# Block attention scores in 64x64 tiles, sums in three groups, later sums in the order, and norm scaling on GpSimd

## The reference

```
x = layernorm(x + blocksparse_attention(x))      # 16 heads of 8, blocks of 64 tokens
hn = layernorm(x)*g + b ; q,k,v = hn@wq+bq, ...   # 16 heads of 8, full 1024x1024 scores
x1 = x + attention(q,k,v)@wo + bo
hn2 = layernorm(x1)*g + b ; idx = argmax(hn2@gate_w + gate_b)
x = layernorm(x + x1 + expert[idx](hn2))
```

## Time and profile before

| | |
|---|---|
| median of 3 runs | 940.32 us (936.14 to 944.61) |
| profiled execution | 937.35 us, its span 935.6 us |
| busy share of the span | PE 81%, DVE 60%, ACT 47%, POOL 22% |
| mean granted PE clock | 0.788 |
| chain that ended last | PE 65%, DVE 18%, issue 5%, POOL 4%, ACT 4%, DMA 3% |

### The profile page before, as it was taken

One profiled execution on the slowest core, in us unless ns is written; L12 is line 12 of the kernel. 1 busy time (PEld: TensorE's weight loads), 2 busy tenths in 40 slices (PEclk: granted clock), 3 DMA queues, 4 the chain that ended last, 5 costly groups with the idle time before them and its releaser, 6 DMA issues.

```text
span 935.6 us, 17249 instructions
## 1 busy us (share of the span) xinstructions
PE 762.3 (81%) x6594; PEld 343.4 (37%) x6594; DVE 565.6 (60%) x941; ACT 443.0 (47%) x826; POOL 203.7 (22%) x460
## 2 busy tenths in 40 slices
PE   4299999999999999977789999987999987305950
PEld 2135655556555565531122212131212122205950
DVE  3253344334554344579987899979789941623745
ACT  2024233333334334327767787866777886002621
POOL 5213420000223342011213410002100000063650
PEclk9557676658657776569989999999999999556985
DMA  4411111212111111111101111110111124013103
GB/s 120 67 18 19 19 19 19 26 19 30 19 19 19 19 19 19 19 15 18 17 10 17 18 22 22 26 14 11 16 18 20 18 78 126 0 40 87 34 32 90
DMA packets 28699, 28.88 MB, mean 31 GB/s; under 512 B 4592, under 2 KB 23824, under 8 KB 28624
## 3 DMA queue, kind: packets, MB, share of 16 engines
q1 hardware_dynamic: 27216, 24.96, 15.4%
q0 software_dynamic: 1408, 2.89, 0.9%
HBM read 9.35 MB, written 5.53 MB: 16 GB/s over the span
## 4 chain that ended last, share of the span: by engine, by line
PE 65%; DVE 18%; issue 5%; POOL 4%; ACT 4%; DMA 3%; SPq 1%; POOLq 0%; ACTq 0%; DVEq 0%
PE PO L1101 23%; PE RB L1138 22%; PE EX L1146 11%; DVE NM L874 11%; ACT PR L732 3%; PE EX L1058 2%; POOL sorted_rows L661 2%; PE RB L1190 1%; PE RB L1115 1%; POOL results L681 1%; PE EX L1197 1%; DVE ST L823 1%; DMA QKT<-QS 1%; PE RB L1089 1%; DVE X L843 1%
## 5 line engine op out<-in xcount | busy, mean ns | idle before, releaser
L874 DVE TENSOR_REDUCE NM<-RB 128x1 f32<-128x1024 f32 (+2 forms) x416 | 433.2, 1067 | 239.7 <-PE RB L1138 229.7
L732 ACT ACTIVATE PR<-EX 128x512 f32<-128x512 f32 (+1 forms) x736 | 383.1, 586 | 300.2 <-PE EX L1146 299.0
L1138 PE MATMUL RB<-QKT 48*128 48x512 bf16 (+4 forms) x1248 | 313.2, 339 | 55.8 <-DVE NM L874 35.5
L1146 PE MATMUL EX<-QKT 51*128 51x512 bf16 (+2 forms) x1536 | 305.6, 309 | 10.3 <-ACT PR L732 6.9
L1101 PE MATMUL PO<-PR,VB 128*32 128x512 f32 (+3 forms) x3072 | 253.1, 440 | 0.1
L1138 PEld LDWEIGHTS RB<-QKT 48*128 48x128 bf16 (+1 forms) x1248 | 94.0, 103 | 286.1 <-DVE NM L874 142.9
L1146 PEld LDWEIGHTS EX<-QKT 51*128 51x128 bf16 (+1 forms) x1536 | 99.4, 111 | 114.7 <-ACT PR L732 69.5
L1101 PEld LDWEIGHTS PO<-PR,VB 128*32 128x32 f32 x3072 | 94.6, 128 | 51.0 <-issue 35.8
L637 POOL COPY VB<-VST 128x128 f32<-128x128 f32 (+1 forms) x64 | 18.7, 292 | 340.4 <-PE PO L1101 327.7
L647 POOL CAST MS<-NM 128x16 bf16<-128x16 f32 x32 | 6.3, 198 | 169.3 <-DVE NM L874 142.0
L755 ACT COPY QS<-QS 128x1156 f32 x12 | 13.8, 1155 | 57.8 <-DVEq L965 43.1
(11 more groups left out here) (158 smaller groups left out, 510.7 us busy)
## 6 DMA issues: line engine op xcount, KB each, us to landing
QKT<-QS SPq DMA_DIRECT2D x64, 192.0 KB
QS<-in_L_ffn_w_dram SPq DMA_DIRECT2D x1, 2048.0 KB, 9.3
QS<-in_L_ffn_w_dram SPq DMA_DIRECT2D x4, 512.0 KB, 9.5
sorted_rows<-PR SPq DMA_DIRECT2D x3, 516.0 KB, 10.1
QKT<-sorted_rows SPq DMA_DIRECT2D x3, 516.0 KB, 5.6
QKT<-MT SPq DMA_DIRECT2D x64, 6.0 KB
CTX<-results SPq DMA_DIRECT2D x2, 512.0 KB, 5.1
X<-_attn_hidden_states_dram SPq DMA_DIRECT2D x2, 384.0 KB, 4.1
```

Of the source, the lines that this page charges most:

```text
L732: nc.scalar.activation(PR[:, at % RING, h, 0:n], bank(key)[:, 0:n], ACT.Exp).then_inc(s_aread, 1)
L874: nc.vector.tensor_reduce(NM[v % 2][:, h, tiles[0]:tiles[-1] + 1], ps, AX_X, ALU.max, negate=True).then_inc(s_dread, 1)
L1138: ins = pe.matmul(spread(ps[r0:r1, c:c + of[1] * of[3]], of), columns(v, h, 0, ROWS6, (l0, 1, 0, ln)), columns(v, h, 1, ROWS6, of), start= ...
L1146: ins = pe.matmul(spread(ps[r0:r1, c:c + of[1] * of[3]], of), columns(xv, xh, 1, ROWS9, (l0, 1, 0, ln)), columns(xv, xh, 0, ROWS9, of), st ...
```

## The change

- Block layer: each MAX matmul of 128 queries becomes two of 64 queries (array columns 0 to 63, and 64 to 127), and the 64-wide window pieces are joined with their neighbours where the columns of `QKT` allow it. Each EXP matmul that was 128 wide becomes two of 64. All score matmuls of that layer are 64x64.
- Block layer: the last three of five groups of sums become one, behind the last EXP step.
- Both layers: `ready` is one beat later. In the full layer the sums so stand between the two beats of a pair.
- SCALE goes from DVE to POOL for the five passes inside the attention layers (40 instructions); DVE keeps the last one.
- A wait of EXP for a free slot of `PR` now names the last group that reads it.

```diff
--- before.py
+++ after.py
@@ -1,4 +1,6 @@
 from contextlib import ExitStack
+
+from itertools import zip_longest
 
 import numpy as np
 
@@ -85,16 +87,29 @@
 
     L = Layer()
     t7 = (TT - 1) * P
-    L.max_acts = [dict(tiles=(0,), n=1024, mms=[(ALL, k * 512, (0, P), (k * 512, 1, 0, 512)) for k in range(2)])]
+
+    def window(j, off, col):
+
+        blk, rows = 2 * j + off // BLK, UPP if off else LOW
+        query, c = (j * P + off, BLK), block_col(blk)
+        if j == TT - 1:
+            near = [(P, (block_col(13), 1, 0, P) if off == 0 else (block_col(2), 2, block_col(1) - block_col(2), BLK))]
+        elif block_col(blk - 1) == c - BLK:
+            near = [(P, (c - BLK, 1, 0, 3 * BLK))]
+        else:
+            near = [(P, (block_col(blk - 1), 1, 0, BLK)), (P + BLK, (c, 1, 0, 2 * BLK))]
+        return [(rows, col, query, (0, 1, 0, P))] + [(rows, col + c0, query, of) for c0, of in near]
+
+    def turns(f):
+
+        return [m for pair in zip_longest(f(0), f(BLK)) for m in pair if m]
+
+    L.max_acts = [dict(tiles=(0,), n=1024, mms=[(LOW if off == 0 else UPP, k * 512, (off, BLK), (k * 512, 1, 0, 512))
+                                                for k in range(2) for off in (0, BLK)])]
     for j in range(1, TT - 1, 2):
-        L.max_acts.append(dict(tiles=(j, j + 1), n=320, mms=[m for i in (0, 1) for m in [
-            (ALL, 512 * i, ((j + i) * P, P), (0, 2, (j + i) * P, P)),
-            (LOW, 512 * i + 2 * P, ((j + i) * P, BLK), (block_col(2 * (j + i) - 1), 1, 0, BLK)),
-            (UPP, 512 * i + 2 * P, ((j + i) * P + BLK, BLK), (block_col(2 * (j + i) + 2), 1, 0, BLK))]]))
-    L.max_acts.append(dict(tiles=(TT - 1,), n=256, mms=[
-        (ALL, 0, (t7, P), (0, 1, 0, P)),
-        (LOW, P, (t7, BLK), (block_col(13), 1, 0, P)),
-        (UPP, P, (t7 + BLK, BLK), (block_col(2), 2, block_col(1) - block_col(2), BLK))]))
+        L.max_acts.append(dict(tiles=(j, j + 1), n=320, mms=[m for i in (0, 1) for m in turns(
+            lambda off: window(j + i, off, 512 * i))]))
+    L.max_acts.append(dict(tiles=(TT - 1,), n=256, mms=turns(lambda off: window(TT - 1, off, 0))))
 
     def single(j, col):
 
@@ -121,6 +136,9 @@
                 [m for j in range(1, 5) for m in single(j, 2 * P + (j - 1) * BLK)])
     ends = dict(n=P, mms=[m for j in (5, 6) for m in single(j, (j - 5) * BLK)])
     L.exp_steps = [first[0], odd, first[1], even, own, rest, ends]
+    for st in L.exp_steps:
+        st["mms"] = [half for rows, c, (l0, ln), of in st["mms"] for half in
+                     ([(LOW, c, (l0, BLK), of), (UPP, c, (l0 + BLK, BLK), of)] if rows == ALL else [(rows, c, (l0, ln), of)])]
     L.exp_acts = [(0, 1), (2, 3), (4, 5), (6,)]
 
     def both(f):
@@ -135,12 +153,12 @@
                                          (h, 0, 2, (2 * P, P), "full", 6, 0), (h, 1, 3, (448, BLK), "low", t1, 448),
                                          (h, 0, 2, (3 * P, P), "full", 7, 0), (h, 1, 3, (448, BLK), "upp", TT - 1, 448),
                                          (h, 0, 3, (0, 384), "full", 0, P)])),
-        dict(last=4, mms=both(lambda h: [(h, j % 2, 4, ((j - 1) * P, P), "full", j, j // 2 * P) for j in range(1, 5)])),
-        dict(last=5, mms=both(lambda h: [(h, j % 2, 5, ((j - 5) * P, P), "full", j, j // 2 * P) for j in (5, 6)] +
-                              [x for a, b_ in ((1, 2), (3, 4))
-                               for pair in zip(single_v(h, 5, a, 2 * P + (a - 1) * BLK),
-                                               single_v(h, 5, b_, 2 * P + (b_ - 1) * BLK)) for x in pair])),
-        dict(last=6, mms=both(lambda h: [x for pair in zip(single_v(h, 6, 5, 0), single_v(h, 6, 6, BLK)) for x in pair]))]
+        dict(last=6, mms=both(lambda h: [(h, j % 2, 4, ((j - 1) * P, P), "full", j, j // 2 * P) for j in range(1, 5)]) +
+             both(lambda h: [(h, j % 2, 5, ((j - 5) * P, P), "full", j, j // 2 * P) for j in (5, 6)] +
+                  [x for a, b_ in ((1, 2), (3, 4))
+                   for pair in zip(single_v(h, 5, a, 2 * P + (a - 1) * BLK),
+                                   single_v(h, 5, b_, 2 * P + (b_ - 1) * BLK)) for x in pair]) +
+             both(lambda h: [x for pair in zip(single_v(h, 6, 5, 0), single_v(h, 6, 6, BLK)) for x in pair]))]
     L.kinds = ["full", "low", "upp"]
     return L
 
@@ -214,7 +232,7 @@
                 acts.append((beats[i], 4, "EXP", li, u, (j, h)))
                 i += 1
             for e in steps:
-                ready[e] = beats[i + 1] + 0.4
+                ready[e] = beats[i + 2] + 0.4
         acts += [(ready[gr["last"]], 5, "AV", li, u, g) for g, gr in enumerate(L.av_groups)]
         exp_end.append(ready[L.av_groups[-1]["last"]] + 0.2)
         if u % 2:
@@ -415,7 +433,7 @@
 
         def av_group_of(li, e):
 
-            return [i for i, gr in enumerate(LAYERS[li].av_groups) if gr["last"] >= e][0]
+            return max(i for i, gr in enumerate(LAYERS[li].av_groups) if any(m[2] == e for m in gr["mms"]))
 
         def piece(li, b, k):
 
@@ -614,6 +632,12 @@
                     n = 2 * u + k if li == 1 else 4 + u
                     pool.wait_ge(s_var, n + 1)
                     root_steps(pool, nc.gpsimd, s_newton, 4 * ROOT_STEPS * n, VE[:, 0:TT], RD[:, 0:TT], SD[:, 0:TT])
+                if kind == "SCALE" and (li, u) != (2, 1):
+                    src, dst = ((X, X1[:]), (X1, X[:]))[k[0]] if li == 1 else (X, HN2[:, :, 0:HS])
+                    for t in (2 * k[1], 2 * k[1] + 1):
+                        g = u * TT + t
+                        nc.gpsimd.tensor_scalar(dst[:, g, :], src[:, g, :], MV[:, t, 0:1], RD[:, t:t + 1],
+                                                ALU.subtract, ALU.mult).then_inc(s_norm, 1)
                 if kind == "AFFINE" and (li, u) != (2, 1):
                     n, row = (2 * u + 1, 0) if li == 1 else (4 + u, 2)
                     if li == 1 and u == 0:
@@ -828,19 +852,15 @@
                         dve.wait_ge(s_dve, chain[0])
                         link(nc.vector.tensor_scalar(VE[:, 0:TT], MV[:, 0:TT, 1], EPS, None, ALU.add))
                         root_guess(VE[:, 0:TT], RD[:, 0:TT], SD[:, 0:TT]).then_inc(s_var, 1)
-                if kind == "SCALE":
-                    n, src, dst = 2 * u + k[0], (X, X1)[k[0]], (X1, X)[k[0]]
-                    if li == 2:
-                        n, dst = 4 + u, HN2[:, :, 0:HS]
-                    if (li, u) != (2, 1):
-                        dve.wait_ge(s_newton, 4 * ROOT_STEPS * (n + 1))
-                    elif k[1] == 0:
+                if kind == "SCALE" and (li, u) == (2, 1):
+                    n = 4 + u
+                    if k[1] == 0:
                         dve.wait_ge(s_var, n + 1)
                         root_steps(dve, nc.vector, s_dve, chain[0], VE[:, 0:TT], RD[:, 0:TT], SD[:, 0:TT])
                         chain[0] += 4 * ROOT_STEPS
                     for t in (2 * k[1], 2 * k[1] + 1):
                         g = u * TT + t
-                        nc.vector.tensor_scalar(dst[:, g, :], src[:, g, :], MV[:, t, 0:1], RD[:, t:t + 1],
+                        nc.vector.tensor_scalar(HN2[:, g, 0:HS], X[:, g, :], MV[:, t, 0:1], RD[:, t:t + 1],
                                                 ALU.subtract, ALU.mult).then_inc(s_norm, 1)
                 if kind == "AFFINE" and (li, u) == (2, 1):
                     dve.wait_ge(s_norm, TT * (4 + u) + 4 * k + 4)
```

## The result

| | before | after |
|---|---|---|
| median, same chip | 938.39 us (4 runs) | 866.64 us (860.91 to 871.08, 4 runs) |
| ratio | | 0.9222, 95% interval 0.915 to 0.9295 |
| profiled execution, its span | 937.35, 935.6 us | 871.08, 869.3 us |

What follows compares the result with a forecast made beforehand. PE's list was taken to bound the block layer, and PE, DVE and ACT together the full layer. Terms -72 - 2 + 3 - 3 - 6 = -80 us against 937.35 gave 857, forecast 860 us; range 836 to 900.

Steps and rivals of the forecast that it cites:

- PE's list sets the block layer: Block layer before the change: 53 shape changes at 0.12 us plus 19,200 columns give 17.4 of a unit's 18.83 us.
- its 11.6: Block layer rival: PE alone sets the unit at 11.6 us, 72 us less, 788; chance 1%.
- The load takes over as the bound at 10.9 us from MT to MAX: Block layer, first stretch of a unit: loads issued behind the MT copies keep it at 10.9 us or more.
- The size of it: Block layer: 15 units of 16.4 us plus 6 us for four heavy units, 252 instead of 324, minus 72 us.
- The second stretch near the low clock: Block unit from MAX to the next MT: 5.0 us, near the low level since PE has just idled; 6.85 before.
- The low clock stays (rival, 881): Block layer rival: PE idles for the load, clock stays low, 17.8 us a unit, 21 us more; chance 14%.
- Between the layers: +3 forecast: Between the layers: MAX 64x128 alternating with EXP 64x64 adds 6,300 columns and loses 15 shape changes, plus 3 us.
- Sums in the full layer: -3 forecast: Full layer: later sums save a little under 0.3 us a unit at MT, nothing in the loop; minus 3 us.
- Norms: -6 forecast: Full layer: scalings leave DVE, 4.9 us in twelve beats plus 1.1; 0.36 us each on POOL; minus 6 us.
- Matmul issue as the bound (rival, 902): Block layer rival: at 0.066 us an instruction a unit takes 19.2 us, 42 us more; chance 3%.
- Sums starving DVE in the full layer (rival, 980): Full layer rival: sums between the beats make each pair wait 1.0 us, 120 us more; chance 4%.
- Before the first MT: -2 forecast: Before the block layer: 13 MAX steps lose 31 shape changes (3.7 us), of which DVE allows 2; minus 2 us.

Runs made afterwards that it cites:

- E1: Kernel before, with only the block layer's MAX and EXP matmuls made 64x64 as in the change: 879.22 us.
- E3: Changed kernel with the loads planned 9.5 instead of 6.0 ahead, so on SP they stand before the MT copies: 828.50 us.
- E10: Changed kernel with early loads, halved MAX matmuls in the first full unit and the block layer's sums in five groups: 793.2 us.
- E7: Kernel before, with the loads planned 9.5 instead of 6.0 ahead: 940.84 us, ratio 1.001 to 1.009.
- E6: Changed kernel with the block layer's sums in five groups again: 863.13 us.
- E5: Changed kernel with the MAX matmuls of the full layer's first unit also cut into 64-wide halves: 849.98 us.
- E2: Changed kernel with all norm scalings back on DVE: 870.88 us.
- E4: Changed kernel with the sums at their old beat in both layers: 878.10 us.
- E8: Changed kernel with early loads, halved MAX matmuls in the first full unit and the first norm's scalings on DVE: 814.58 us.
- E9: Changed kernel with early loads and halved MAX matmuls in the first full unit, scalings as in the change: 819.62 us.

## Why the prediction was right, point by point

- **PE's list sets the block layer, and array shapes are its cost.** Shown in the main: E1 changes nothing but the tiles and gains 57.8 of the layer's 59.6 us. How much of it is shape changes, how much columns and how much the clock (0.66 before, 0.72 in E1) is not taken apart. The count of columns and shapes holds to 1.1 us of PE's busy time in the unit of the earlier trace rows, but falls 2.2 us short at full clock (E3, E10), so that E3's 11.38 us meets its 11.6 by luck.
- **The load takes over as the bound at 10.9 us from MT to MAX.** Shown by the unit above (10.89) and by E3 and E7 together: the same edit takes 38 us from the change and none from the kernel before. Six of the fourteen first stretches came in at 10.8 to 10.9.
- **The size of it.** -72 was forecast, -59.6 came, and the failing term is the pair of stretches: 10.9 and 5.5 us were taken, 11.56 and 5.98 were measured as means over 14 units. That is 1.1 us a unit, 17 in all, of which the separate term for heavy units (6) covered a part. A cost that the forecast did not have is PE waiting for DVE (17.9 us over the layer, 3.5 before). I had let DVE bound only the second stretch, and had not asked what the merged sums do to it. E6 shows that they cause it: with five groups 17.9 us became 4.5. But E6's layer is only 3.3 us shorter, 261.3 for the 252 forecast, so this cost explains a small part of the shortfall as long as loads bind, and most of it stays open. In one of the units the load itself landed late, 12.3 us behind MT; POOL held PE once for 2.8 us.
- **The second stretch near the low clock.** Right: 5.32 us at 0.50 for 5.0 expected. E3's unit, whose second stretch ran at 1.00 in 4.01 us, shows that the work behind the wait does not need the low clock. My reason, "since PE has just idled", fits these two units but not the unit before the change, at 0.50 with hardly any idle time ahead.
- **The low clock stays (rival, 881).** Partly so. The clock over the layer was 0.74, between 0.66 and the 0.86 of the earlier trace rows, and a clean unit took 16.2 and not 17.8 us. Four of fifteen units took 16 to 17 us as expected, four up to 17.3, the others 17.6 to 20.3.
- **Between the layers: +3 forecast, +8.0 measured.** The mechanism was named and mis-sized. Of the added columns I took 2.6 to 5.2 us and gave back 1.8 for shapes over three units; but in the one unit from MT 15 to 16 both grow, columns by 8,064 and changes of shape by 14, and it ran at clock 0.56: 8,064/1,344 + 14 x 0.12 = 7.7 us. The unit grew by 7.8 us (33.59 to 41.36), though its clock fell as well, from 0.60. E5 takes away that and more.
- **Sums in the full layer: -3 forecast.** Between E1 and E2, which differ in them and in the groups, it is -6.9, and putting them back (E4) costs 5.4. The spot was right (MT), and the loop between two sums is unchanged as forecast (2.46 us). What I left out is the unit with an OT, which gains 0.64 instead of 0.3; what the move does in the units with norms was not looked at apart.
- **Norms: -6 forecast.** In the full layer about that (E2: 6.0, within 4.4 to 7.3). But a scaling on POOL was put at 0.36 us between two rows, and is 0.79, outside both bounds (0.29 and 0.43). I wrote "nothing there" for the block layer; the profiles have 3.9 and 2.8 us against the move there and behind it (E2), and E8 and E9 5 us, each within the spread. For the move in all the medians have 4.2 us, with intervals (0.915 to 0.930, 0.927 to 0.936) that overlap. What it costs outside the full layer stays open.
- **Matmul issue as the bound (rival, 902).** Excluded at its price of 0.066 us: E3's unit runs some 290 matmuls and their loads in 11.38 us, 0.039 us each. A smaller cost of each matmul is not excluded. The Trainium skill, "TensorE: Matmul & The Clock Gate" (Part 1), has about 62 ns for each matmul where the sequencer decodes in software; that would be 18.0 us for this unit, and the trace does not show such a bound.
- **Sums starving DVE in the full layer (rival, 980).** Did not happen: clean units take 20.35 us, 0.3 less than before. But the same mechanism was at work in the block layer, where I had not looked for it.
- **Before the first MT: -2 forecast, -0.7 measured.** From the first MAX matmul to MT 0 it was 12.53 us for 13.65, 1.1 of the 2; but it began 0.4 us later.
- **The range of my own case, 843 to 878, does not follow** from its ends of 14.5 and 17.8 us a unit: over 15 units they give 832 and 881.

The errors partly cancel: the block layer and the passage fell short by 12 and 5 us, the full layer gave 4.5 more. Against the profiled execution the forecast was 14 us off (857 for 871.08); that 860 comes within 7 us of the median is luck in part, since the median was put 3 us above the profiled execution and lay 4.4 below it. The changed kernel gets most of its 8% from its tiles (E1: 6%), and three small edits of its order, its seam and its grouping bring 73 us more.

## What to carry to other kernels

When the engine that sets a stage gets cheaper, look for the transfer that was hidden by just so much, and move its issue ahead of the small copies in front of it before counting the gain. An edit that measures as nothing behind such a bound (E6) must be tried again once the bound is gone (E10): there it was worth 26 us. And a change of tile shape belongs to both sides of every place where two lists of matmuls alternate; at the seam, where only one side had changed, it cost 8 us, and the fix (E5) gave 17.

## What the runs showed of the hardware

- A change of array shape costs 0.10 to 0.14 us of PE's time in the earlier trace rows. E1 has 43 of them fewer in a unit (53 to 10), 5.2 us at 0.12, and gained 3.9 a unit with waits for loads of 25.9 us over the layer that were not there before. The Trainium skill, "TensorEngine Tiling (Array Packing)" (Key Properties), says that changing the tiling mode drains the engine; the 0.10 to 0.14 us fit that.
- Matmuls of one shape on different parts of the array start together, and some start ahead of others that stand before them in the list. RB and EX matmuls alternate in the list here, and still two EX matmuls start, at 105.91, ahead of the RB matmul between them. In the changed kernel, behind MT:

```profile
105.77 0.24 PE L1158 MATMUL RB<-QKT 48*64 48x128 bf16 x1
105.77 0.24 PE L1166 MATMUL EX<-QKT 51*64 51x128 bf16 x1
105.77 0.24 PE L1158 MATMUL RB<-QKT 48*64 48x128 bf16 x1
105.78 0.24 PE L1166 MATMUL EX<-QKT 51*64 51x128 bf16 x1
...
105.91 0.22 PE L1166 MATMUL EX<-QKT 51*64 51x128 bf16 x2
105.94 0.22 PE L1158 MATMUL RB<-QKT 48*64 48x128 bf16 x2
```

- A subtract-and-multiply of 128x128 f32 with two operands per partition takes 0.79 us on POOL, 2.7 times a copy of that size (0.29), and 0.26 on DVE (0.51 for two in the earlier trace rows).
- In the changed kernel's unit the clock read 0.96 while PE worked with short gaps, and 0.50 behind a gap of 3.35 us. The wait cost its length and then some of the next work at half speed: 3.35 us less of idling went with 4.83 us less of time in the pair of units above.
- The low clock also comes without idle time: it was 0.66 over the block layer before, with PE busy 98% of it, and 0.56 in the unit from MT 15 to MT 16 of the changed kernel, with PE busy for 39.58 of 41.36 us. With 14 changes of shape in that unit instead of 53 (E5) it was 0.88. So a list full of shape changes ran at a low clock here although PE counts as busy; what the clock goes by is not shown.
